# Layer 0: weight, bias and y's modulated u from VectorE to ScalarE

## The reference, cut to what matters

```python
xn = _ln(x, ln_w, ln_b)                       # (x - m) * rsqrt(v + eps) * w + b
q = softmax(xn @ Wq + bq, over a head's channels)
k = softmax(xn @ Wk + bk + mask, over tokens)
v = (xn @ Wv + bv) * mask
y = q @ (k^T v)                               # per head
hh = _ln(y, ln2_w, ln2_b) * (1 + scale) + shift   # scale, shift from the embedding
x = x + silu(hh) @ W_out + b_out
```

## Time and profile before

| | |
|---|---|
| times of three runs | 1315.82, 1318.12, 1322.36 us; median 1318.12 |
| the profiled execution's own time | 1315.51 us |
| its span, first to last instruction | 1313.7 us |
| mean granted TensorE clock | 0.979 of full speed |
| busy, share of the span | PE 96%, DVE 77%, ACT 69%, POOL 38% |
| of 231 to 264 us (33 us, in layer 0) | PE 31.41, DVE 30.23, ACT 11.97, POOL 11.15 us busy |

### The profile page before, as it was taken

How to read it: one execution, slowest core, us unless ns; L and a number is a source line. 1 busy time by engine, 2 the same in 40 slices (tenths; PEclk the granted TensorE clock), 3 DMA queues, 4 the chain that set the end, 5 groups by cost and what they waited for, 6 DMA issues and landing times.

```text
span 1313.7 us, 24811 instructions
## 1 busy us (share of the span) xinstructions
PE 1255.7 (96%) x9256; PEld 996.7 (76%) x9256; DVE 1016.4 (77%) x2027; ACT 907.4 (69%) x2051; POOL 497.2 (38%) x451
## 2 busy tenths in 40 slices
PE   8997999999999989999999999999999999999998
PEld 6776878778787778567787787787787787787666
DVE  5778787988979768567877877877877877877766
ACT  5323424324243536888898998998998998998884
POOL 0426356383664551000531631621621620721602
PEclk8988999999999999999999999999999999999989
DMA  9244464745646646774555555555555555554512
GB/s 332 81 153 126 124 200 113 232 126 171 195 117 202 185 147 192 223 228 130 162 170 154 168 173 146 181 168 141 184 170 148 183 165 152 178 163 145 167 45 81
DMA packets 123081, 214.13 MB, mean 163 GB/s; under 512 B 8704, under 2 KB 38456, under 8 KB 122064
## 3 DMA queue, kind: packets, MB, share of 16 engines
q1 hardware_dynamic: 122960, 212.55, 52.8%
HBM read 130.14 MB, written 81.85 MB: 161 GB/s over the span
## 4 chain that ended last, share of the span: by engine, by line
PE 55%; DVE 15%; POOL 13%; ACT 12%; issue 3%; DMA 1%; SPq 0%; DVEq 0%; POOLq 0%; ACTq 0%
PE ps L615 12%; PE ps L617 11%; PE ps L616 11%; PE ps L797 7%; PE ps L771 6%; ACT ps L962 5%; PE ps L779 4%; ACT Pb L972 4%; POOL wr L1413 3%; POOL sTh L1426 3%; POOL sTl L1428 2%; DVE xTl L1107 2%; DVE cT L1248 2%; PE ps L610 2%; PE ps L722 2%
## 5 line engine op out<-in xcount | busy, mean ns | idle before, releaser
L962 ACT ACTIVATE ps<-ps,cT 128x512 f32<-128x512 f32 x512 | 345.6, 722 | 27.7 <-DVE cT L1248 26.8
L1248 DVE TENSOR_REDUCE cT<-ps 128x1 f32<-128x512 f32 x512 | 322.1, 682 | 35.8 <-PE ps L771 33.3
L972 ACT ACTIVATE Pb<-ps 128x512 f32<-128x512 f32 x512 | 279.0, 628 | 16.5 <-PE ps L779 14.6
L771 PE MATMUL ps<-Ks,Qs 98*128 98x512 f32 x512 | 188.5, 427 | 7.0 <-ACT ps L962 4.6
L779 PE MATMUL ps<-Qs,Ks 100*128 100x512 f32 x512 | 172.0, 407 | 3.6 <-ACT ps L962 1.7
L771 PEld LDWEIGHTS ps<-Ks,Qs 98*128 98x128 f32 x512 | 96.2, 192 | 61.6 <-ACT ps L962 30.3
L962 ACT ACTIVATION_READ_ACCUMULATOR ps<-ps,cT 128x1 f32 x512 | 137.3, 268 | 0.0
L615 PE MATMUL ps<-xTh,Wh_k 128*128 128x512 f32 x256 | 108.7, 425 | 22.9 <-DVE xTl L1107 19.3
L779 PEld LDWEIGHTS ps<-Qs,Ks 100*128 100x128 f32 x512 | 95.8, 189 | 42.2 <-ACT Pb L972 9.3
L615 PE MATMUL ps<-Wh_o,sTh 128*128 128x512 f32 x256 | 103.2, 403 | 7.4 <-POOL sTl L1428 5.5
L1384 POOL TENSOR_SCALAR vf<-vf,mk 128x512 f32<-128x512 f32 x16 | 25.1, 1566 | 214.9 <-DVE vf L1158 214.9
(11 more groups left out here) (178 smaller groups left out, 2765.8 us busy)
## 6 DMA issues: line engine op xcount, KB each, us to landing
Qs<-stack_scratch SPq DMA_DIRECT2D x32, 768.0 KB
Ks<-stack_scratch SPq DMA_DIRECT2D x32, 768.0 KB
stack_scratch<-sg_q SPq DMA_DIRECT2D x32, 512.0 KB, 2.7
stack_scratch<-sg_k SPq DMA_DIRECT2D x32, 512.0 KB, 2.7
wr<-in_x SPq DMA_DIRECT2D x32, 256.0 KB, 5.1
x_scratch<-wr SPq DMA_DIRECT2D x32, 256.0 KB, 3.8
stack_scratch<-sg_q SPq DMA_DIRECT2D x32, 256.0 KB, 2.9
stack_scratch<-sg_k SPq DMA_DIRECT2D x32, 256.0 KB, 3.3
```

What stands on the lines that cost most here:

```text
L771: e.matmul(bank[:], Qs[par][0:RX, j, t * 128:(t + 1) * 128], Ks[par][0:RX, j, :], start=True, stop=True).then_inc(s["S"], 1)
L962: e.activation(bank[:], bank[:], ACT.Exp, bias=nx[:, n % 2, j, t, 0:1], accum_out=dn[:, b % 2, t, 4 * g + j:4 * g + j + 1]).then_inc(s["S_ ...
L972: e.activation(Pb[m][:, j, :], ps[bank_of["a", n, m, j]][:], ACT.Exp).then_inc(s["P"], 1)
L1248: e.tensor_reduce(nx[:, n % 2, j, t, 0:1], ps[bank_of["S", n, j, t]][:], AX.X, ALU.max, negate=True).then_inc(s["S_max"], 1)
```

## The change

In `tx` of batches 1 to 7, ACT waits for POOL's `xn` instead of DVE's `x_f`, and writes `xTh` with the weight as its scale and the bias as its bias. A second ACT instruction then writes the full value in place into `xr` and signals `x_f`. DVE's L1102 is gone. Its subtraction waits for `x_f` of its own tile, and stands in the second half of each tile's step instead of one tile later in the first half.

In `ty` of batches 0 to 7, ACT makes u right behind its tanh. DVE's L1214 is gone there, and L1219 waits for ACT's `y_ua`. In batches 8 to 14 DVE still makes u; batch 15 is as before.

```diff
--- before.py
+++ after.py
@@ -265,6 +265,11 @@
     return x < 7
 
 
+def u_by_act(x, c):
+
+    return x < 8 or x == 15 and c % 2 == 1
+
+
 def in_bank(x):
 
     return x >= 7
@@ -852,8 +857,10 @@
                             e.wait_ge(s["qk_mm"], 8 * (x - 8))
                             e.wait_ge(s["v_mm"], 4 * x)
                     if turned_on_host(x):
-                        e.wait_ge(s["x_f"], 4 * (x - 1) + c + 1)
-                        e.copy(xTh[:, c, :], xr[:, c, :]).then_inc(s["xT_hi"], 1)
+                        p = cols[0]
+                        e.wait_ge(s["xn"], 4 * x + c + 1)
+                        e.activation(xTh[:, c, :], xr[:, c, :], ACT.Identity, scale=p[:, c:c + 1], bias=p[:, 4 + c:5 + c]).then_inc(s["xT_hi"], 1)
+                        e.activation(xr[:, c, :], xr[:, c, :], ACT.Identity, scale=p[:, c:c + 1], bias=p[:, 4 + c:5 + c]).then_inc(s["x_f"], 1)
                         return
                     if c == 0 and x % 8 == 0:
                         e.wait_ge(s["l_cols"], 32)
@@ -928,7 +935,7 @@
                     w, u = at.stop - at.start, u_tile(x, c)
                     scale, bias = mod[:, 0, ch, x % 8:x % 8 + 1], mod[:, 1, ch, x % 8:x % 8 + 1]
                     e.activation(tb[c % 2][:, 0:w], u[:, 0:w], ACT.Tanh, scale=scale, bias=bias).then_inc(s["y_tanh"], 1)
-                    if x == 15 and c % 2:
+                    if u_by_act(x, c):
                         e.activation(u[:, 0:w], u[:, 0:w], ACT.Identity, scale=scale, bias=bias).then_inc(s["y_ua"], 1)
                 if i == 1 and c:
                     c -= 1
@@ -1029,7 +1036,7 @@
                 if h == 0:
                     e.wait_ge(s["be1"], L + 1)
                     if L:
-                        e.wait_ge(s["y_u"], 32)
+                        e.wait_ge(s["y_ua"], 32)
                 e.wait_ge(s["et"], 2 * L + h + 1)
                 for c in range(NC):
                     e.tensor_scalar(mod[:, h, c, :], src[:, c, :], add[:, c:c + 1], 0.5, ALU.add, ALU.mult).then_inc(s["e_mod"], 1)
@@ -1096,15 +1103,10 @@
                     e.tensor_scalar(nm[:, 1, :], mv[:, 1, :, 0], -1.0, None, ALU.mult).then_inc(s["y_nm"], 1)
 
             def tx(i, x, c):
-                if i == 0 and turned_on_host(x):
-                    p = cols[0]
-                    e.wait_ge(s["xn"], 4 * x + c + 1)
-                    e.tensor_scalar(xr[:, c, :], xr[:, c, :], p[:, c:c + 1], p[:, 4 + c:5 + c],
-                                    ALU.mult, ALU.add).then_inc(s["x_f"], 1)
                 if turned_on_host(x):
-                    for u in ((c - 1,) if i == 0 and c else (3,) if i == 1 and c == 3 else ()):
-                        e.wait_ge(s["xT_hi"], 4 * x + u + 1)
-                        e.tensor_tensor(xTl[:, u, :], xr[:, u, :], xTh[:, u, :].bitcast(F32), ALU.subtract).then_inc(s["xT_lo"], 1)
+                    if i == 1:
+                        e.wait_ge(s["x_f"], 4 * (x - 1) + c + 1)
+                        e.tensor_tensor(xTl[:, c, :], xr[:, c, :], xTh[:, c, :].bitcast(F32), ALU.subtract).then_inc(s["xT_lo"], 1)
                     return
                 if i == 1:
                     e.wait_ge(s["xT_f"], tx_count(x, c))
@@ -1210,12 +1212,12 @@
                         e.wait_ge(s["y_tanh"], n)
                         if 8 <= x < 15 and c == 0:
                             e.wait_ge(s["o_mm"], 4 * x)
-                        if x < 15 or c % 2 == 0:
+                        if not u_by_act(x, c):
                             e.tensor_scalar(u, u, mod[:, 0, ch, bb:bb + 1], mod[:, 1, ch, bb:bb + 1],
                                             ALU.mult, ALU.add).then_inc(s["y_u"], 1)
-                            e.wait_ge(s["y_u"], n if x < 15 else 61 + c // 2)
+                            e.wait_ge(s["y_u"], n - 32 if x < 15 else 29 + c // 2)
                         else:
-                            e.wait_ge(s["y_ua"], 1 + c // 2)
+                            e.wait_ge(s["y_ua"], n if x < 8 else 33 + c // 2)
                         e.scalar_tensor_tensor(out=s_tile(x, c), in0=tok(x, tb[c % 2][:, 0:w]), scalar=1.0, in1=tok(x, u),
                                                op0=ALU.add, op1=ALU.mult).then_inc(s["y_s"], 1)
                     if c and (x < 8 or x == 15):
```

## The result

The changed kernel took 1298.66 us (median of 4 runs, 1298.25 to 1302.19) against 1319.27 for the kernel before (median of 4, 1315.82 to 1322.36). The ratio is 0.985 with an interval of 0.982 to 0.987: about 20 us, or 1.5%, faster. The forecast was 1302 in a range of 1294 to 1314.

A forecast was written before the change was run, and what follows sets the result against it. PE, busy 96%, was taken as the bound, with 19.3 us of layer 0 waits for xTl; 8.0 + 2.4 + 2.0 + 1.6 + 2.3 - 0.5 = 15.8 us gave 1299.7 from the profiled run, 1302 for the median, range 1294 to 1314.

The forecast's parts named there:

- The like borders: Batches 3 to 7: both PE waits for xTl go, 1.6 us gained each, 8.0 in all (3.5 to 9.5).
- With nothing to spare: Batch 4's last tile: subtraction ends at 234.5 to 234.9, PE wants it at 235.05; POOL is its clock.
- Batches 1 and 2: Their borders: batch 1 gains 2.4 us (1.2 to 4.0); batch 2 gains 2.0, its 4.77 us wait staying.
- The clock behind batch 3: TensorE at 0.50 speed from 181 to 184 us returns to full as the waits go: 1.6 us (0 to 1.6).
- The y steps in layer 0: ACT's block of four tiles takes 8.5 us, as long as before: cost 0, with DVE's 3.26 us idle as cover.
- the slower rival: ACT's y block stretches and stops PE in eight batches; decides at 13.8 us; at 15 us, 1328; chance 0.07.
- The end of layer 0: Batch 6's y steps: ACT's quicker u ends PE's 2.33 us wait before L722; gain 2.3 us (0 to 2.5).
- The 0.5 that was counted for batch 7's u: Batch 7's y steps, ahead of layer 1's exponentials: more work on ACT costs 0.5 us (0 to 2).
- What ACT's instructions cost: Layer 0: about 60 more activations at 0.75 us, 45 us; scaled high part 0.1 us above the plain copy.
- Layer 1 "moves earlier as a whole": Layer 1: instructions stay the same and their lists move earlier as a whole; no term in the sum.
- POOL does set the last tile: Rival, POOL sets the pace at the borders: 0.7 us gained at each, 7.7 in all, 1310; chance 0.18.
- The rival of more, 1297: Borders of batches 1 and 2: the clock comes back too, 4 to 5 us more, 1297; chance 0.12.

The follow-up runs named there:

- its further pass: Changed kernel, but POOL goes once more over the last of four x tiles per layer 0 batch before handing it over: 1309.11 us, ratio 0.994.
- x's half alone: Changed kernel with y's u put back on VectorE in layer 0, only x's part of the change left: 1301.20 us, ratio 0.988 to before.
- the late subtraction: Changed kernel with VectorE's subtractions back where they stood before, one tile late: 1296.17 us, ratio 0.984 to before.
- two more tanhs: Changed kernel in which ScalarE writes each tanh of layer 0 three times instead of once: 1346.72 us, ratio 1.022 to before.
- the y half: Changed kernel with x's weight and bias back on VectorE, subtractions one tile late, only u left on ScalarE: 1314.18 us, ratio 0.999 to before.

## Why the prediction was right, and where it was not

**The like borders: right.** Both waits went in batches 3 to 7, and ACT's pair, DVE's addition and the last subtraction came in the order that was worked out. Each gave 1.9 us, where 1.6 was forecast and 1.9 named as the most, since the restarted matmuls (0.50 instead of 0.40) go too. That is 9.6 against 8.0. "With nothing to spare" holds for POOL, by the kernel with its further pass; on ACT 0.5 us were to spare.

**Batches 1 and 2: right, with the clock undersized.** Batch 1 gave 3.3 against 2.4. Its waits fell by 1.9, from 4.01 to 2.07; the rest is the clock, 0.69 from 70 to 78 us before and 0.84 after. Batch 2 gave 2.1 against 2.0; the wait of 4.77 stayed as said, at 4.54. Of the 2.1, 1.6 is the last tile's step, which came sooner, and 0.6 is clock that the forecast had not counted: the matmuls behind that step follow each other every 0.23 us, where the first four before stood 0.43 apart. The whole stretch, 115.3 to 124.3 us, still reads only 0.72, against 0.51 in the earlier trace rows.

**The clock behind batch 3: right.** From 170 to 180 and from 180 to 188 the row now reads 1.00, where the earlier trace rows had 0.50 in one stretch. Columns as there:

```profile
170.00:180.00 10.00, 10.00 (x49) 8.11 (x48) 7.94 (x20) 1.72 (x3) 8.16 (x7) 1.00 0.81 307
180.00:188.00 8.00, 8.00 (x37) 6.64 (x36) 7.69 (x24) 4.16 (x10) 0.00 (x0) 1.00 0.73 213
```

**The y steps in layer 0: the price of nothing was right, the cover was read on one way only.** ACT's block ran from 240.44 to 248.84, 8.4 us against 8.5 forecast. DVE went to the v additions 24.7 us after batch 4's first k matmul, against 26.8 before; without the 1.6 us of border waits that is half a microsecond sooner:

```profile
247.49 0.69 DVE L1221 SCALAR_TENSOR_TENSOR eraw<-tb,eraw 128x512 f32<-128x512 f32 x1
248.10 1.46 DVE L1227 TENSOR_TENSOR sTl<-eraw,sTh 128x512 fp32r<-128x512 f32 x2
249.48 1.89 DVE L1160 TENSOR_TENSOR ps<-ps,bvB 128x512 f32<-128x512 f32 x3
```

The failed step is that the cover of 3.3 us, read from DVE's idle time before the next q part, was taken for the whole of it. I followed the block only to the v additions and the banks, and there it was right: with a block of 15.0 us PE waited 3.1, where the slower rival said 3.2. But the block also stands ahead of the y copies, and so of POOL's queue and of the next border. The cover is 1.6 us there, and the slower rival decides at a block of 11.7 us and not of 13.8: with 3.25 us added the kernel was level with before. At 15.0 us it lost 49 us against the changed kernel, where the rival's sum had 26.

**The end of layer 0: the wait went, but not by ACT's u alone.** The wait before the second y product is gone, which moved the matmuls by 2.5 us at that point (forecast 2.3). With x's half alone it fell to 0.77: VectorE's u, which took 2.54 us beside POOL before, took 0.79 there, and the stretch from 406 to 480 gave 1.8 us. So in these traces ACT's u took away only the last 0.8 us of the 2.3. In the profiled run 1.5 us were lost just before it. Some 0.4 of that is the wait before the first y product, 3.03 us where it was 2.58: ACT's copy for it stood behind a cast that waited for a weight. The other 1.1 is the clock, which behind that wait stayed low longer. Four microseconds from the same matmul of the q product on, before and changed (16 matmuls against 11), and ACT's rows:

```profile
466.40:470.40 4.00, 4.00 (x16) 3.19 (x16) 3.93 (x4) 1.34 (x2) 3.85 (x4) 0.86 0.00 0
451.00:455.00 4.00, 4.00 (x11) 3.08 (x11) 3.74 (x3) 4.00 (x7) 3.85 (x4) 0.51 0.00 0
```

```profile
447.62 0.62 ACT L832 CAST Wh_q<-sp 128x512 fp32r<-128x512 f32 x1 [1.79 <-DMA sp<-in_Wq]
448.14 0.58 ACT L917 COPY qT<-ps 128x512 f32<-128x512 f32 x1
448.62 0.59 ACT L923 COPY yb<-ps 128x512 f32<-128x512 f32 x1
```

In the kernels with the late subtraction and with batch 7's u on VectorE that wait was 2.3 and 2.5 us, not 3.03, and the stretch gave 3.6 and 4.0 us instead of 1.4. The 0.5 that was counted for batch 7's u is too small for the ratios to confirm or refute.

**What ACT's instructions cost: right.** ACT was busy for 46.8 us more, where 45 were forecast. One reading in it was off: a high part with scale and bias takes 0.82 us where the plain copy took 0.62 to 0.63, so 0.2 more, and not the 0.1 of the estimate: it has two such operands, a scale and a bias. That POOL would regain a few tenths does not show in its sum: it was busy for 497.2 us before and 498.1 after.

**Layer 1 "moves earlier as a whole": wrong.** The twelve kernels here that came early to layer 1 lost 1.0 to 3.6 us between 520 and 600 us of before's time, and 0.3 to 1.3 us later. The same matmuls, to within a few, first before, then changed:

```profile
559.50:572.60 13.10, 10.79 (x90) 6.13 (x94) 9.98 (x24) 10.86 (x32) 0.98 (x2) 1.00 1.03 315
```

```profile
543.00:558.00 15.00, 12.64 (x94) 7.59 (x98) 10.55 (x27) 11.82 (x33) 0.73 (x1) 0.77 0.90 273
```

The clock was 1.00 in the one and 0.77 in the other, and the same work took 15.0 us instead of 13.1, which is nearly all of the 2.2. The clock fell in this stretch, to 0.77 to 0.88, in all twelve; in the kernel with two more tanhs, which came 29 us late, it stayed at 1.00. Why it fell was not tested and stays open.

**The sum.** The terms were 15.8 and measured 9.6 + 3.3 + 2.1 + 1.6 + 1.4 = 18.0. The trace lost 3.5 of it in layer 1 and 1.2 at the start, which leaves 13.3; the other runs, spans 3.4 to 3.9 us shorter, were back near the terms. So the total owes something to luck: layer 0 gave 2.2 us more than its terms, and layer 1, which stood in no term, took more than that away. None of the rivals came: POOL does set the last tile, but just in time, so that it took nothing from the borders. The rival of more, 1297, came in part: some of batch 1's clock returned and little of batch 2's.

## What to carry to other kernels

Ask of each edit which instruction is last at the wait that it is to end. 26 us taken from VectorE gave 16 us where they stood ahead of that instruction, and 23 us gave nothing that can be measured where they did not. Follow a lengthened block through every engine's queue to each point where TensorE may stop, not only along the instructions behind it; here the way over POOL to the next border had half the cover of the way that was read. When a border's last step hangs on three engines, moving it forward on one or two of them gained nothing here, and moving the whole chain gained 6.6 us in the trace, half of which went to the next transfer in the queue.

## What the runs showed of the hardware

- Behind a border the granted clock fell or did not fall on small differences. Waits of 0.85 and 0.73 us at batch 6 of the kernel before left it at 1.00, and waits of the same two lengths at its batch 3 (178.52 and 180.21 us) were followed by 0.50 from 181 to 184. Waits of 1.80 and 0.74 at batch 6 of the y half brought it to 0.60 for 4 us, which cost about 1.7 us on top of 0.95 of longer wait. So there one microsecond of wait had nearly the price of three.
- ACT's high part with scale and bias took 0.80 to 0.82 us alone, but the next began 0.71 later, so a pair alone took 1.5 us from start to end (224.19 to 225.71) and pairs in a row 1.4 each. The forecast had 0.75 an activation.
- POOL's added pass of a tile took 1.50 us, and handed the tile over 1.6 us later with its semaphore; the border was 1.6 us late, all of it.
- A load that waits for its own stores holds up what stands behind it in SP's queue: q's load was issued at 141.65 behind it, and at 136.11 without it.
